# A graph network with routed experts: the sort's type one-hots read 128 columns wide

## What is computed

```python
def _message_passing(h, src, tgt, et, Wq, bq, Wk, bk, Wv, bv, Ee, Wo, bo, n_nodes):
    Q = (h @ Wq.T + bq).reshape(-1, H, DH)
    K = (h @ Wk.T + bk).reshape(-1, H, DH)
    V = (h @ Wv.T + bv).reshape(-1, H, DH)
    scores = jnp.einsum('ehd,egd->ehg', Q[src], K[tgt]) / jnp.sqrt(jnp.float32(DH))
    attn = jax.nn.softmax(scores, axis=-1)
    msg = jnp.einsum('ehg,egd->ehd', attn, V[tgt]).reshape(-1, HID)
    msg = msg + Ee[et]
    proj = msg @ Wo.T + bo
    return jax.ops.segment_sum(proj, src, num_segments=n_nodes)
```

## Time and profile before

| | us |
|---|---|
| median of three runs (3537.24 to 3538.97) | 3538.44 |
| the profiled execution | 3541.01 |
| its span in the trace | 3539.2 |
| PE busy | 3271.6 (92%) |
| DVE busy | 2490.4 (70%) |
| ACT busy | 2416.9 (68%) |
| POOL busy | 2371.5 (67%) |

### The profile page before, as it was taken

One profiled execution on the slowest core, in us unless ns is written; L12 is line 12 of the kernel. 1 busy time (PEld: TensorE's weight loads), 2 busy tenths in 40 slices (PEclk: granted clock), 3 DMA queues, 4 the chain that ended last, 5 costly groups with the idle time before them and its releaser, 6 DMA issues.

```text
span 3539.2 us, 82782 instructions
## 1 busy us (share of the span) xinstructions
PE 3271.6 (92%) x24455; PEld 2776.6 (78%) x24456; DVE 2490.4 (70%) x7379; ACT 2416.9 (68%) x5342; POOL 2371.5 (67%) x2552
## 2 busy tenths in 40 slices
PE   6999969999999898999999989999999998779998
PEld 3555459888888767888888876888888886679998
DVE  9888878788777756877777774777777788821111
ACT  3677658778777667877777756777777774334443
POOL 3656667777777757777777775777777776534443
PEclk9999979999999999999999999999999999889999
DMA  2111067777777537777777744777777775366664
GB/s 83 40 43 40 30 202 212 211 212 212 212 211 211 150 132 221 211 212 211 211 211 211 212 131 146 212 211 212 211 212 212 211 211 179 118 187 181 186 184 113
DMA packets 264839, 621.15 MB, mean 176 GB/s; under 512 B 85199, under 2 KB 129158, under 8 KB 256391
## 3 DMA queue, kind: packets, MB, share of 16 engines
q0 software_dynamic: 161376, 477.59, 48.5%
q1 hardware_dynamic: 103351, 142.22, 12.2%
HBM read 570.22 MB, written 49.62 MB: 175 GB/s over the span
## 4 chain that ended last, share of the span: by engine, by line
PE 42%; issue 19%; POOL 15%; DMA 14%; DVE 7%; ACT 1%; POOLq 1%; DVEq 0%; SPq 0%; ACTq 0%
POOL arena L607 15%; DMA arena<-kv_d,gidx 13%; PE bank L1743 7%; PE bank L1901 6%; PE bank L1913 5%; PE bank L1717 4%; PE bank L1732 3%; PE bank L1693 2%; PE bank L1589 2%; PE bank L1710 2%; PE bank L1660 2%; PE bank L1597 1%; PE bank L1687 1%; PE bank L1652 1%; PE bank L1658 1%
## 5 line engine op out<-in xcount | busy, mean ns | idle before, releaser
L607 POOL DMA_INDIRECT arena<-kv_d,gidx x1764 | 1683.7, 954 | 614.3 <-issue 529.9
L1743 PE MATMUL bank<-att,arena 128*128 128x128 f32 x7056 | 934.2, 276 | 15.7 <-DVE att L968 15.5
L1732 PE MATMUL bank<-qbd,kt_s 128*128 x7056 | 935.3, 276 | 0.3 <-ACT kt_s L1393 0.2
L1743 PEld LDWEIGHTS bank<-att,arena 128*128 128x128 f32 x7056 | 856.8, 192 | 21.1 <-DVE att L968 20.4
L1732 PEld LDWEIGHTS bank<-qbd,kt_s 128*128 128x128 f32 x7056 | 861.6, 193 | 1.1 <-issue 1.1
L939 DVE TENSOR_REDUCE sc<-bank 128x32 f32<-128x512 f32 x882 | 607.1, 688 | 314.1 <-PE bank L1732 301.2
L1717 PE MATMUL bank<-ident,arena 128*128 128x128 f32 x3528 | 684.2, 286 | 96.8 <-DMA arena<-kv_d,gidx 73.5
L1393 ACT ACTIVATE kt_s<-bank 128x512 f32<-128x512 f32 x882 | 525.0, 595 | 357.4 <-PE bank L1717 349.2
L1401 ACT ACTIVATE bank<-oh,bigc 128x512 f32<-128x512 bf16 x882 | 604.9, 686 | 47.7 <-PE bank L1765 22.7
L968 DVE TENSOR_TENSOR att<-bank,oh 128x512 f32<-128x512 f32 x882 | 601.9, 683 | 27.2 <-PE bank L1743 1.2
L1717 PEld LDWEIGHTS bank<-ident,arena 128*128 128x128 f32 x3528 | 403.6, 142 | 265.0 <-DMA arena<-kv_d,gidx 254.3
(11 more groups left out here) (248 smaller groups left out, 3863.2 us busy)
## 6 DMA issues: line engine op xcount, KB each, us to landing
arena<-in_pack SPq DMA_DIRECT2D x56, 1030.0 KB, 5.1
arena<-kv_d,gidx POOLq DMA_INDIRECT x1764, 3.7
kv_d<-arena SPq DMA_DIRECT2D x75, 256.0 KB, 2.0
hid_d<-arena SPq DMA_DIRECT2D x75, 128.0 KB, 2.0
xin<-hid_d SPq DMA_DIRECT2D x75, 128.0 KB, 2.1
arena<-in_w SPq DMA_DIRECT2D x8, 1024.0 KB, 8.3
oh<-oh_d SPq DMA_DIRECT2D x219, 32.0 KB
rec_d<-arena POOLq DMA_INDIRECT x241, 2.1
```

The costliest lines, as they stand in the source:

```text
L607: pool.indirect_dma_start(kv[:, t // UB, t % UB, :], None, kv_d, bass.IndirectOffsetOnAxis(gidx[:, h, t - h * HT:t - h * HT + 1], 0),).the ...
L1732: ins = mm(bk[:, :].rearrange("p (g t n) -> p t g n", g=H, t=2)[:, u, 2 * c:2 * c + 2], kt_s[:, p % 2, u, c, :], qbd[:, p // QP % 2, ds(w, ...
L1743: ins = mm(bank[6 + p // QP % 2][:, o:o + P], kv[:, b, u, D + g * DH:D + (g + 2) * DH], att[:, b % 2, u, :, g:g + 2, :].rearrange("p s g h ...
```

## The change

The one-hots of types get 64 places per column in place of 48, with one more column per buffer, and all of it is zeroed once at the start. The matmul of the counts reads 128 adjacent places as its stationary operand: the 64 of its own column and the 64 of the next. Its first 48 result rows are the counts as before; the others hold sums that nothing reads. All lines behind the first added one are one later in the changed kernel, those behind the memset two.

```diff
+SW = 64
...
-        n_win, n_sy = 2 * CH * NW, 2 * CH * SY
+        n_win, n_sy = 2 * CH * NW, 2 * (CH + 1) * SW
...
-        oh_sy = early_b[:, n_win:n_win + n_sy].rearrange("p (b k n) -> p b k n", b=2, k=CH)
+        oh_sy = early_b[:, n_win:n_win + n_sy].rearrange("p (b k n) -> p b k n", b=2, k=CH + 1)
...
             link(dve.memset(hi_f[:, EC:], float(HI)))
+            link(dve.memset(oh_sy[:, :, :, :], 0.0))
             link(dve.memset(wl_f[:, EC:], float(LO)))
...
-                    oh_sy[:, b, 0:n, :], iotab[:, 0:SY].unsqueeze(1).to_broadcast([P, n, SY]),
+                    oh_sy[:, b, 0:n, 0:SY], iotab[:, 0:SY].unsqueeze(1).to_broadcast([P, n, SY]),
...
-                    mm(bank[2][0:SY, 2 * EX:2 * EX + NW], oh_sy[:, b, k, :], oh_win[:, b, k, :], start=False, stop=(n == 1), skip_group_check=True)
+                    mm(bank[2][:, 2 * EX:2 * EX + NW], oh_sy[:, b, k:k + 2, :].rearrange("p k n -> p (k n)"), oh_win[:, b, k, :], start=False, stop=(n == 1), skip_group_check=True)
```

## The result

| | before, us | after, us |
|---|---|---|
| median | 3537.84 (3534.38 to 3538.97, 4 runs) | 3491.31 (3489.46 to 3495.41, 4 runs) |
| profiled execution | 3541.01 | 3489.46 |
| its span | 3539.2 | 3487.6 |

The ratio is 0.9872, with a 95% interval of 0.9855 to 0.9889: 46.5 us less, where 37.5 were forecast. The time is 0.7 us under the range given; that ratio times the 3538.44 us from which the forecast started is 3493.1, which lies inside it. Medians are of the fast runs; one run of ten of the kernel of the first experiment, at 8024 us, is not in its median.

The account below looks back on a forecast made before the run. PE was taken to bound the sort's steady chunks, with DVE next. Chunk gains of 38.4 us less 0.85 for the zeroing gave 37.5 us off 3538.44, forecast 3501.0 us, range 3492 to 3515 (about 0.8).

Parts of the forecast that it names:

- The bound and the gaps: Sort, 48-wide matmul of the counts: PE bounds, losing 0.09 us ahead of it and 0.11 behind, 2.7 us a chunk.
- The gain ends at DVE: Steady sort chunks: DVE is next, own list 11.1 us; chunk falls from 13.62 to 12.14, 34.0 us over 23 chunks.
- The price behind the wide operand: Seven of 13 sort steps go on with an f32 matmul: gap taken as 0.11 us, f32 piece staying 0.96.
- the lower end named there: Same gap ahead of f32 matmuls, at the least: nothing beyond the 0.09 us or less, giving an 11.8 us chunk.
- Chunk 2: Sort's chunk 2, at first at TensorE's lower level: about six steps lose some 0.25 us each, 1.0 us gained.
- chunk 27: Sort's chunk 27, by the same lists with fewer f32 pieces: 1.5 us gained.
- The zeroing: DVE memset of 896 words ahead of the first one-hots: 0.80 us and 0.04 for its link, 0.85 lost.
- The covers: POOL's wait for DVE falls from 3.17 to 1.7 us, 0.6 in the last full chunk; ACT's 9.65 fit into 12.14.
- both sides went: Against the rival that only entry or exit gap goes: 12.6 to 12.7 us a chunk, 3514 us, chance 0.10.
- the pitch gave nothing: Against the rival that gaps belong to the place in the program, not the width: 3539.3 us, chance 0.06.
- a load of 128 columns: Against the rival that the wider load is exposed and grows, entry gap 0.24 us: some +50 us, 3590, chance 0.05.
- DVE alone sets the pace: Rival for the sort's chunks: PE's slack absorbs the f32 pieces, 11.1 us a chunk, 3476 us, chance 0.04.

Follow-up runs that it names:

- the first experiment: The changed kernel with the operand of the counts 48 columns wide again, pitch and zeroing kept: 3538.77 us, ratio 1.0006.
- the pair of narrow matmuls: The kernel before with a second 48-wide matmul, on a block of zeros, added ahead of each one of the counts: 3557.04 us in a single run.
- the kernel with the moved pieces: The kernel with the covers, plus f32 pieces for keys and values moved to steps 4 and 5, permutations to 2, 3, 6, 9, 11: 3469.27 us, the fastest.
- the kernel with the covers: The changed kernel with the zeroing ahead of DVE's wait for the edges and ACT's copy of the queries behind the first one-hot operations: 3482.95 us.
- the kernel before with the moved pieces: The kernel before, 48 wide, with keys and values moved to steps 4 and 5, permutations to 2, 3, 6, 9, 11: 3524.16 us, ratio 0.9977.

## Why the prediction was right, and where not

**The bound and the gaps: right.** Both gaps went, in all 13 steps, and came back with 48 columns alone. Whether the load or the switch costs it was left open; in the pair of narrow matmuls the second costs next to nothing, so it is the switch.

**The gain ends at DVE: right.** PE's busy time fell by 2.9 us and the chunk by 1.8. DVE's own list was put at 11.1, with five waits of which one was counted twice; with four the same rule gives 11.52 - 4 x 0.08 = 11.2. The chunk that hardly waits for PE, in the kernel with the moved pieces, takes 11.2.

**The price behind the wide operand: the term that was mis-sized.** "f32 loads follow each other by (0.52 - 0.19) / 3 = 0.11; that is the nearest row, and I take 0.11", with the pieces left at 0.96. Measured are 0.09 to the piece and 0.88 for it. So the lower end named there, the row of 0.96 already holding a load that could start earlier, was the true one: the lists gave 11.8 for it and 11.81 is measured, against the 12.14 taken. 23 x 0.33 = 7.6 us of the 9 that the forecast fell short. The load rows above show why the nearest row misled: the first load of the f32 piece had waited for the switch.

**Chunk 2: mis-sized, and not by the width alone.** It gives 1.6 us in place of an estimated 1.0. But in the kernel of the first experiment, with 48 columns again, it takes 11.64 us (60.74 to 72.38), 0.96 less than before; with 96 columns it takes 11.57. It depends on when TensorE leaves the lower of its levels. The first matmul with `below` that lasts 0.25 us, where those ahead of it last 0.35 to 0.37, stands at 66.03 us in the kernel before, at 63.94 with 48 columns again and at 63.62 in the changed kernel. In the four kernels with one narrow matmul a step, that moment comes 3.2 to 6.0 us after the first scatter of chunk 1, and chunk 2 grows with it from 11.64 to 12.60 us. What sets it is not shown. That the 0.6 us too much here and the 0.7 too little of chunk 27 cancel is luck.

**The zeroing: right in kind, 1.1 in place of 0.85.** DVE's timeline at the start:

```profile
4.92 0.06 DVE L729 MEMSET arena<- 128x1 f32 x1 [2.02 <-DMA iotab<-in_c_iota]
5.23 0.81 DVE L730 MEMSET arena<- 128x896 uint32 x1 [0.25 <-DVE arena L729]
6.10 0.06 DVE L731 MEMSET arena<- 128x1 f32 x1
```

The 0.81 is what was taken from the earlier trace rows, but the link before it adds 0.25. The first scatter of chunk 1 is still only 0.7 later: from L732 (L730 before) to DVE's first reduction it takes 25.4 us where it took 25.8, and why is not shown.

**The covers: one wait not foreseen.** POOL stayed behind DVE as said, 1.63 us in the steady chunks and 0.78 before the last. But chunk 27 takes 12.58, where 11.5 was expected by the lists for the kernel with the covers. ACT stood 4.00 us before its copy of the queries, released by a DMA, the store of the last group of input rows (`xb_d`). From its timeline (the copy, and the hidden state that was late behind it), and from PE's, which waited for that:

```profile
355.78 1.99 ACT L1320 ACTIVATE arena<-bank,bq 64x128 f32<-64x128 f32 x4 [4.00 <-DMA xb_d<-arena]
...
362.63 0.38 ACT L1344 ACTIVATE xT<-bank 128x256 f32<-128x256 f32 x1
```

```profile
363.07 0.71 PE L1608 MATMUL bank<-xT,wq 128*128 128x128 f32 x4 [1.56 <-ACT xT L1344]
```

From its issue to its landing the store took 5.4 us here. In the kernel before it took 3.6, from 393.14 us on, and ended 0.2 us ahead of ACT's copy at 396.93. So the longer chunks only just covered it, and its own time decides: with 96 columns, at the same pace and with the copy in the same place, it took 3.7 us and chunk 27 11.56. In the kernel before with the moved pieces it took 5.3, and ACT stood 3.75 us in spite of chunks of 13.37. So the slow store costs the changed kernel about 1 us, once. A slow one with the copy moved stands only in the fastest kernel (5.4 us): its chunk 27 takes 11.23, no longer than the steady ones.

**The rivals.** Each is out: both sides went, the pitch gave nothing, and a load of 128 columns takes no longer than one of 48 (means of 98 and 99 ns in the steady chunks). The Trainium skill's rule on LDWEIGHTS ("TensorE: Matmul & The Clock Gate", section on LDWEIGHTS), a load time by columns, brought nothing on the slower side: between 48 and 64 columns the entry doesn't change, and 128 columns are hidden behind a stream of 200. The load rows don't follow that rule either: 99 ns for 48 columns, 106 for 64, 123 for 96 and 98 for 128. DVE alone sets the pace only once the f32 pieces are moved.

## What to carry to other kernels

Look at the distance from one matmul's start to the next against its columns: where one narrow matmul stands among full-width ones and both its neighbours are late by a fixed amount, widen it, with zeros or with a neighbour's data, until it is of their kind (here 96 columns were enough and 64 were not). Price the gain by the engine that is next, laying both engines' lists side by side step by step; and then move the long pieces of the one to where the other has long ones. When a loop becomes shorter, look for transfers that were only just covered: the same store took 3.4 to 5.4 us in the runs here, and whether a chunk was late hung on that.

## What the runs showed that I had not expected

An f32 piece gets shorter by 0.08 us (0.96 to 0.88 for keys and values, 0.55 to 0.47 for queries) when the matmul ahead of it is of the full width: the cost of the switch reached into the duration of the piece behind it, whose first load started late, and no gap shows it.

POOL stops twice with no releaser shown: after the 113th scatter (the first of chunk 14) and after the 226th (the second of chunk 28). The first stop takes 3.00 us in both kernels, and POOL's waits for DVE cover nearly all of it. The second takes 4.17 us in the kernel before and 3.74 in the changed one:

```profile
383.62 0.96 POOL L590 DMA_INDIRECT rec_d<-arena  x1 [3.74 <-issue]
```

Both move with the scatter's number and not with time: they stand behind the same two scatters in all ten kernels (the second for 3.00 to 4.25 us). The scatters behind the second run without a pause to the last, so it lies on the path; its cause wasn't looked for.
